# A transformer layer with a routed expert stage: unused products on TensorE before the first and after the last expert chunk

## The reference

```python
# attention, 16 heads of 64, and a residual
q, k, v = x @ Wq, x @ Wk, x @ Wv
attn = softmax(q @ k.T * (1 / (64 * 64 * 16)))
x = layernorm(x + (attn @ v) @ WO)
# experts: 8 of them, each token goes to its best two
probs = softmax(x @ gate_W); w, idx = top_k(probs, 2); w = w / w.sum()
out = 0.5 * gelu(x @ shared_W + shared_b)
for e in range(8):
    out += combine[:, e:e+1] * (gelu(x @ W1[e] + b1[e]) @ W2[e] + b2[e])
out = (out - mean) * rsqrt(var + 1e-5) * gamma + beta
x = layernorm(x + out)
```

## Time and profile before

| what | value |
|---|---|
| median of three runs | 1809.6 us (1808.56 to 1811.19) |
| the profiled execution, its own time | 1826.84 us |
| its span, first to last instruction | 1825.1 us |
| PE busy | 1730.8 us, 95% |
| DVE, ACT, POOL busy | 75%, 56%, 21% |
| mean granted TensorE clock | 0.981 |

### The profile page before, as it was taken

How to read it: one execution, slowest core, us unless ns; L and a number is a source line. 1 busy time by engine, 2 the same in 40 slices (tenths; PEclk the granted TensorE clock), 3 DMA queues, 4 the chain that set the end, 5 groups by cost and what they waited for, 6 DMA issues and landing times. The chain is left out here.

```text
span 1825.1 us, 31876 instructions
## 1 busy us (share of the span) xinstructions
PE 1730.8 (95%) x10919; PEld 1186.5 (65%) x10919; DVE 1373.6 (75%) x2218; ACT 1025.7 (56%) x1529; POOL 380.3 (21%) x422
## 2 busy tenths in 40 slices
PE   6999999999999999999999999799579999999977
PEld 5555555555555555555555554688579999999972
DVE  5888888888888888888888888666656655566647
ACT  5565555655556565565555555466545554555537
POOL 1000000000000000000000000016247666666664
PEclk9999999999999999999999999899889999999998
DMA  5011111111111111311111111465223333233335
GB/s 178 30 35 43 39 37 41 36 36 41 42 36 36 42 41 36 131 36 39 38 41 36 36 41 36 140 216 181 92 77 92 86 89 89 45 87 87 91 59 171
DMA packets 80197, 127.09 MB, mean 70 GB/s; under 512 B 12752, under 2 KB 46736, under 8 KB 77776
## 3 DMA queue, kind: packets, MB, share of 16 engines
q1 hardware_dynamic: 61808, 98.27, 16.3%
q0 software_dynamic: 18272, 27.31, 7.5%
HBM read 86.72 MB, written 38.83 MB: 69 GB/s over the span
## 5 line engine op out<-in xcount | busy, mean ns | idle before, releaser
L447 ACT ACTIVATE a_e<-banks 128x1024 f32<-128x1024 f32 x512 | 483.4, 1033 | 262.3 <-PE banks L344 262.3
L558 DVE TENSOR_TENSOR a_esum<-a_esum,a_e 128x1024 f32<-128x1024 f32 x384 | 470.5, 1225 | 94.6 <-ACT a_e L447 60.8
L358 PE MATMUL banks<-a_e,a_v 128*64 128x512 f32 x2048 | 467.5, 598 | 0.0
L358 PEld LDWEIGHTS banks<-a_e,a_v 128*64 128x64 f32 x2048 | 135.6, 136 | 265.6 <-issue 242.5
L63 POOL MEMSET ident<- 128x128 f32 x1 | 0.2, 205 | 1126.8 <-POOLq L112 1126.8
L344 PE MATMUL banks<-a_qh,a_kh 64*128 64x512 f32 x1024 | 222.2, 428 | 5.7 <-issue 5.3
L344 PE MATMUL banks<-a_qh,a_kl 64*128 64x512 f32 x1024 | 203.9, 390 | 0.0
L344 PE MATMUL banks<-a_ql,a_kh 64*128 64x512 f32 x1024 | 203.9, 392 | 0.0
L1796 ACT ACTIVATE e_g<-banks,e_b1c 128x256 f32<-128x256 f32 x280 | 114.4, 470 | 150.7 <-PE banks L1744 147.3
L344 PEld LDWEIGHTS banks<-a_qh,a_kh 64*128 64x128 f32 x1024 | 97.4, 185 | 144.3 <-issue 97.3
L1757 PE MATMUL banks<-e_w2h,e_hh 128*128 128x256 f32 x560 | 162.3, 290 | 4.9 <-DVE e_hl L1822 2.4
(11 more groups left out here) (237 smaller groups left out, 3314.0 us busy)
## 6 DMA issues: line engine op xcount, KB each, us to landing
attn_out<-a_ot SPq DMA_DIRECT2D x64, 256.0 KB, 2.0
a_inv<-inv_rows SPq DMA_DIRECT2D x126, 128.0 KB, 2.8
a_w<-w_qkv SPq DMA_DIRECT2D x32, 256.0 KB, 3.1
raw<-attn_out SPq DMA_DIRECT2D x4, 2048.0 KB, 8.9
t_ot<-attn_out SPq DMA_DIRECT2D x4, 2048.0 KB, 9.3
raw<-w_up SPq DMA_DIRECT2D x8, 1024.0 KB
raw<-w_down SPq DMA_DIRECT2D x8, 1024.0 KB
raw<-x_t SPq DMA_DIRECT2D x8, 512.0 KB, 9.4
```

Of the source, the lines that this page charges most:

```text
L358: mm = pe.matmul(o_acc[h * DH:(h + 1) * DH, :], v[quad % 2][:, n, head], e[(slot * ST + n) % NE][:, h * BANK:(h + 1) * BANK], start=n == 0 ...
L447: act.activation(e[t % NE], ring[n % RING], ACT.Exp, scale=SCALE).then_inc(e_ok, 1)
L558: dve.tensor_tensor(acc[:, :], acc[:, :], e[(slot * ST + n) % NE], ALU.add).then_inc(add_ok, 1)
```

## The change

At the end of TensorE's program in `tokens`, 24 bfloat16 products of 128 x 512 are added. They use tiles that are there already and write bank 6, which nobody reads. They stand behind the signal `sorted_ok`. At the beginning of TensorE's program in `outputs`, 56 float32 products of the identity with itself, 128 x 128, are added. They write a part of bank 0, and stand ahead of the wait for the first normalised tile. No wait, signal or DMA is added or moved.

```diff
@@ tokens
+    KEEP_AWAKE = 24
@@ tokens, TensorE's program
             sort(3)
             sort(4).then_inc(sorted_ok, 1)
+            for _ in range(KEEP_AWAKE):
+                pe.matmul(banks[6][:, :], low_hot[:, 0, 0, :], low_hot[:, 0, 0:BANK // P, :].rearrange("p a b -> p (a b)"),
+                          start=True, stop=True)
@@ outputs
     LAG = 2
+    KEEP_AWAKE = 56
@@ outputs, TensorE's program
     def tensor(pe):
         flat = lambda rows, t: rows[:, t:t + PAIR, :].rearrange("p t d -> p (t d)")
+        for _ in range(KEEP_AWAKE):
+            pe.matmul(banks[0][:, 0:P], ident[:, :], ident[:, :], start=True, stop=True)
         for t in range(0, TT, PAIR):
```

## The result

The changed kernel takes 1815.75 us in the median of eight runs (1811.77 to 1818.75), the kernel before 1809.08 in the median of eight (1807.9 to 1811.19). The ratio is 1.0031 with a 95% interval of 1.0020 to 1.0043: 5.6 us slower, 3.6 to 7.8.

What follows compares the result with a forecast made beforehand. TensorE, busy 95% of the span, was taken to bound the kernel nearly everywhere. First part 0 plus second part +2.7 us on 1809.6 gave 1812.3 us; the range was 1807.5 to 1815.5.

Steps and rivals of the forecast that it cites:

- The likeliest class: Whole kernel: a time within 0.2% (3.6 us) of before, counted as the same; chance 0.70.
- The first part: Behind the sort: 24 products end at 1335.4, before GpSimd's drain; the clock falls again before `up`; gain 0.
- The bound: At `up`: if the clock holds, chunk 0 ends at 1354.9 instead of 1356.09, a gain of 1.2 us at most.
- The place of the second part's cost: Ahead of the outputs: added products delay the second group of sums to 1792.5, against 1789.79; cost +2.7 us.
- The formula: Second group of sums: TensorE free, plus six products of 0.86 (5.2 us), plus 0.17 for the last one's tail.
- when TensorE is free: Ahead of the outputs: after the added products, at 1785.0 with full clock, 1787.1 with 2.1 us lost to half clock.
- How long the products take: Added products ahead of the outputs: 112 instructions at 0.115 us, 12.9 us, plus 2.1 us lost at half clock.
- When they begin: Added products ahead of the outputs: not before 1772.07, when TensorE's branch ends; about 3.1 us idle before.
- The branch: TensorE's sequencer leaving the chunks: a 4647 ns stall, hidden before, stays and becomes the start of the added work.
- The rival of a bridged gap: Ahead of the outputs: the clock survives the 3.1 us gap, first part worth nothing; +0.6, 1810.2 us; chance 0.20.
- The slower rival: Ahead of the outputs: float32 pairs do not overlap their weight loads; over +5 us, up to +11.7, 1821.3; chance 0.08.
- The faster one: Both places: clock holds for `up`, second part begins soon enough; -1.2 - 0.6 = -1.8, 1807.8 us; chance 0.13.

Runs made afterwards that it cites:

- the kernel that holds it: Against the kernel before: only 36 products behind the sort, plus 10 float32 products between the first transposes and `up`; 0.9994, then 0.9993 on the third chip.
- the nearer one: Second part alone, in a kernel with code for 36 chunks instead of 40 and a slightly narrower sort; one run took 1811.68 us, branch 0.345 us.
- 12 products in front: The whole change with 12 products behind the sort instead of 24; one run took 1810.11 us beside 1809.01 of the kernel before.
- 1.0036: The whole change measured again on another chip, against the kernel before there: 1833.91 us, ratio 1.0036, 6.3 us slower than 1827.62.
- 1.0025: The whole change with the 24 products behind the sort cut from 512 columns to 8, against the kernel before: 1832.38 us, ratio 1.0025.
- 1.0013: Only the 56 products ahead of the outputs, second measurement, against the kernel before on the same chip: 1829.37 us, ratio 1.0013.
- the kernel with 20 products: Only the second part, with 20 products ahead of the outputs instead of 56, against the kernel before: ratio 1.0002.

## Why the prediction was right or wrong

The direction of the likeliest number was right and its size too small: +2.7 us forecast, +5.6 by the ratio measured. The median of 1815.75 lies 0.25 above the top of the range, 1815.5; the ratio put onto the 1809.6 of the prediction gives 1815.2. The likeliest class, within 0.2%, did not come; slower had 0.25. That the result lies at the edge of the range is luck: the range ends at 1813.4 with the longest stretch at half clock, and the 2.1 us above that were allowed for scatter, not for the causes that came.

**The first part** was right. The products end at 1333.3, 3.4 us before GpSimd's drain is over; `up` begins at half clock; alone the part measures 1.0004. When the clock falls was surer in the prediction than it is: the transposes still had it in two of three traces, and the wait for VectorE behind them lost it. The bound, 1.2 us for a clock that holds, is what the kernel that holds it shows: 1.1 and 1.3 in two ratios, neither told from no change, and 1.9 at most in the traces. The stretch at half clock was shorter than before, and no gain from that shows in the time; that VectorE's parts of the Gelu are the reason is argued, not shown.

**The place of the second part's cost** was right: the products end behind the first normalised tile, and three pairs of sums stand behind them. The formula gives the time within 0.02 us: TensorE free at 1770.03, plus 5.2 and 0.17, is 1775.40, and VectorE began at 1775.38. But the wait that it stands for did not come. I had VectorE waiting over 2 us at the second group of sums; it waited 5.08 us at the first group, for two products, and none at the second. From 1771.95 its own work took 3.43 us, and TensorE's four further products take 4 times 0.86, or 3.44, so both paths end at the same moment. That the sum of six products fits is a coincidence: products faster than that would not have helped the second group.

**The term that was mis-sized is when TensorE is free.** Against the landing I had 1787.1 - 1778.7 = 8.4 us, and the trace has 1770.03 - 1758.81 = 11.2. The three parts of the difference of 2.8:

- How long the products take: 16.95 us instead of 15.0. 89 instructions took 9.7 us at full clock, 0.109 each instead of 0.115, so 12.2 in all: -0.7. The other 23 ran at half clock and took 1.66 and 3.75 us instead of 2.5: 2.9 lost and not 2.1, +0.8. The gap in the supply is 1.7, which I did not have at all. (0.15 is left over.) It failed in the step "At 0.115 an instruction, between that and 0.12 of `down`, 112 are 12.9 us", which took the instructions as always there.
- When they begin: 2.8 us behind the last `down` product, not 3.4, as the branch took 3.99 and not 4.65 us: -0.6.
- When the rows land: 8.5 us behind the last `down` product, not 10.0 as in the earlier trace rows: +1.5. I had one trace of before, and took from it a distance that goes from 8.4 to 11.6 over the traces of all kernels; what sets it is open.

**The branch** was read rightly as a stall that was hidden and would show. That its length comes from the distance of its target was argued then, and is borne out now by the nearer one, in one run. What I did not draw from it: behind such a branch the code that follows can be late as well.

**The rivals.** The rival of a bridged gap, +0.6, did not come in the change; its mechanism came once, with 12 products in front. The slower rival, loads that don't overlap, is out: 0.109 us an instruction at full clock. The faster one needed the clock to hold in both places, and in the three traces with all instructions of the change it held in neither.

How much of the 5.6 us each part makes is measured on one chip by 1.0036, 1.0025 and 1.0013. The intervals of the first and the last just don't overlap (from 1.0024, up to 1.0022), that of the middle one overlaps both; that the first part's work, as against its instructions, costs something too (1833.91 against 1832.38) is open.

## What to carry to other kernels

Unused products held TensorE's clock here in the three traces in which they reached from the last real product to the next one, with gaps of about 1.1 us. Over longer gaps the length alone did not decide: the clock outlasted 2.9 and twice 3.7 us, was lost over 2.5 to 3.3 us ahead of the outputs in the other traces, and fell within 1 us behind a gap of 2.1 in three. Count from the trace when they can start, not when the engine falls idle, and let them end before the thing that the engine waits for. A branch over much code and the block behind it are stalls of their own, which show in no wait: look at the branch's duration in the sequencer's rows before putting work behind it. And adding instructions in one place moves the code behind, so two edits that cost little alone (1.0004 and 1.0013) can meet (1.0036): time them together and apart.

## What the runs showed of the hardware that was not expected

- The supply of instructions can stop a second time shortly behind a far branch, at a place that moved by exactly one matrix instruction for each product taken away in front (7 to 19 for 12).
- The clock can outlast one idle stretch and fall after a shorter one. It was full at the transposes 3.73 us (first part alone) and 3.70 us (whole change, second trace) after the last product. Behind a gap of 2.09 us in `tokens` it fell although TensorE was busy again; TensorE behind that gap, and the clock, in the second trace of the whole change:

```profile
1298.26 0.46 PE L1078 MATMUL banks<-raw,t_before 128*128 128x96 f32 x2 [2.09 <-POOLq L996]
...
1298.26:1299.00 0.74, 0.74 (x6) 0.74 (x7) 0.02 (x1) 0.74 (x1) 0.27 (x1) 0.91 0.00 0
1299.00:1302.00 3.00, 2.62 (x8) 1.86 (x7) 2.79 (x13) 1.65 (x5) 1.93 (x3) 0.50 0.60 206
```

- The clock can fall in the middle of the outputs, with TensorE busy all the time by the record: in the kernel with 20 products (columns of the earlier trace rows),

```profile
1792.60:1795.90 3.30, 3.30 (x5) 1.24 (x5) 2.96 (x18) 3.01 (x9) 1.59 (x2) 0.50 0.46 159
```

and likewise in the kernel with code for 36 chunks and in the first part alone, where nothing in the outputs was changed. The outputs behind the landing took 46.8, 48.0 and 47.5 us there, against 45.8 and 46.4 in two traces of before; that the clock makes the difference is not shown.
- The same unchanged kernel had medians of 1809.08, 1822.02, 1827.62 and 1809.01 us in four groups, and the stage of the experts took 420 us in a trace of the group of 1822.02.
